# When a new batch's values are computed: after two turned tiles, and ahead of the rows' turns and logits

## What is computed

```python
q = split_heads(x @ Wq + bq); k = split_heads(x @ Wk + bk); v = split_heads(x @ Wv + bv)
p = softmax(where(causal, q @ k.T / sqrt(32) + alibi, min))
x = layernorm(x + (p @ v) @ Wo + bo)
probs = softmax(x @ Wr + br); top_w, top_idx = top_k(probs, 1)
x = layernorm(x + top_w * expert[top_idx](x))      # silu(x @ Wg) * (x @ Wu) @ Wd
```

## Time and profile before

| | |
|---|---|
| median of 3 runs | 1213.38 us (1212.68 to 1215.46) |
| profiled execution | 1214.71 us |
| its span | 1212.9 us |
| mean granted clock of TensorE | 0.976 |
| TensorE busy | 1149.1 us, 95% |
| VectorE, ScalarE, GpSimd busy | 731.5, 590.4, 518.7 us |

### The profile page before, as it was taken

How to read it: one execution, slowest core, us unless ns; L and a number is a source line. 1 busy time by engine, 2 the same in 40 slices (tenths; PEclk the granted TensorE clock), 3 DMA queues, 4 the chain that set the end, 5 groups by cost and what they waited for, 6 DMA issues and landing times.

```text
span 1212.9 us, 25969 instructions
## 1 busy us (share of the span) xinstructions
PE 1149.1 (95%) x7725; PEld 1028.8 (85%) x7725; DVE 731.5 (60%) x1969; ACT 590.4 (49%) x1485; POOL 518.7 (43%) x666
## 2 busy tenths in 40 slices
PE   7899998999999988999999999999999999999994
PEld 5778877887788766989889989989988998998993
DVE  5566676668667746473654565466365456546665
ACT  3588876876787774342333233233232323323354
POOL 6776764755576564630331231133033123213336
PEclk9899998999999988899999999999999999999997
DMA  8323333233332222532222313213222231321312
GB/s 247 101 62 84 67 88 87 54 75 93 84 77 69 71 62 87 176 95 71 71 70 72 105 44 90 77 54 87 71 69 73 71 105 45 95 72 53 88 37 104
DMA packets 105375, 100.12 MB, mean 83 GB/s; under 512 B 10271, under 2 KB 79519, under 8 KB 105248
## 3 DMA queue, kind: packets, MB, share of 16 engines
q1 hardware_dynamic: 100064, 87.18, 26.7%
q0 software_dynamic: 3040, 9.18, 2.4%
q10 hardware_dynamic: 2144, 2.10, 0.6%
HBM read 64.74 MB, written 9.18 MB: 61 GB/s over the span
## 4 chain that ended last, share of the span: by engine, by line
PE 51%; POOL 5%; DMA 2%; issue 2%; DVE 1%; ACT 1%; SPq 0%; POOLq 0%; ACTq 0%; DVEq 0%
PE bank L976 36%; PE bank L1001 9%; POOL up_lo L1735 5%; PE bank L988 3%; DMA up_raw<-in_Wu_dram 2%; PE bank L704 1%; ACT up_hi L1131 1%; PE bank L950 1%; POOL out_dram L1819 0%; DMA y<-x_scratch,row_token 0%; DVE oT_lo L1335 0%; SPq L628 0%; PE bank L803 0%; PE bank L855 0%; PE bank L931 0%
## 5 line engine op out<-in xcount | busy, mean ns | idle before, releaser
L1735 POOL TENSOR_TENSOR up_lo<-up_raw,up_hi 128x256 fp32r<-128x256 f32 x241 | 171.2, 746 | 481.7 <-ACT up_hi L1131 481.3
L976 PE MATMUL bank<-up_hi,xsT_hi 128*128 x1216 | 355.4, 292 | 7.3 <-POOL up_lo L1735 6.3
L976 PE MATMUL bank<-up_hi,xsT_lo 128*128 x1216 | 343.8, 283 | 0.0
L976 PE MATMUL bank<-up_lo,xsT_hi 128*128 x1216 | 343.7, 283 | 0.0
L1543 DVE SCALAR_TENSOR_TENSOR h_tok<-bank,row_weight,silu 128x128 f32<-128x128 f32 x304 | 93.4, 346 | 292.7 <-ACT silu L1233 292.7
L1726 POOL TENSOR_TENSOR pT_lo<-probs,pT_hi 128x512 fp32r<-128x512 f32 (+1 forms) x192 | 210.5, 1103 | 125.4 <-ACT pT_hi L1108 124.4
L976 PEld LDWEIGHTS bank<-up_hi,xsT_hi 128*128 128x128 f32 x1216 | 232.4, 191 | 14.2 <-issue 13.9
L1233 ACT ACTIVATE silu<-bank 128x256 f32<-128x256 f32 (+1 forms) x160 | 59.9, 374 | 364.3 <-PE bank L976 360.6
L976 PEld LDWEIGHTS bank<-up_hi,xsT_lo 128*128 128x128 f32 x1216 | 233.1, 192 | 0.3
L976 PEld LDWEIGHTS bank<-up_lo,xsT_hi 128*128 128x128 f32 x1216 | 232.7, 191 | 0.1
L1560 DVE TENSOR_TENSOR y<-bank,y 128x512 f32<-128x512 f32 x295 | 198.9, 689 | 0.4
(11 more groups left out here) (196 smaller groups left out, 2087.4 us busy)
## 6 DMA issues: line engine op xcount, KB each, us to landing
stack<-qk SPq DMA_DIRECT2D x180, 128.0 KB, 2.4
up_raw<-in_Wg_dram SPq DMA_DIRECT2D x64, 256.0 KB, 3.8
up_raw<-in_Wu_dram SPq DMA_DIRECT2D x64, 256.0 KB, 4.2
down_raw<-in_Wd_dram SPq DMA_DIRECT2D x64, 256.0 KB
x_tok<-in_x_dram SPq DMA_DIRECT2D x16, 256.0 KB, 3.3
x_scratch<-res SPq DMA_DIRECT2D x12, 256.0 KB, 2.4
w_raw<-in_Wo_dram SPq DMA_DIRECT2D x1, 1024.0 KB, 6.5
stack<-max_row SPq DMA_DIRECT2D x64, 2.0 KB
```

What stands on the lines that cost most here:

```text
L976: mm = pe.matmul(bank[:, n * 2 * P:(n + 1) * 2 * P], a[:, s, k, :], up_w[w][k][:, :, :].rearrange("p a f -> p (a f)")[:, bass.ds(at, 2 * P ...
L1735: pool.tensor_tensor(up_w[1][k][:, e, :], up_raw[:, idx % NUPS, k, :, :].rearrange("p g f -> p (g f)"), up_w[0][k][:, e, :].bitcast(F32), ...
```

## The change

In the planner only, and in the waits that follow from it:

- V needs two turned tiles, those of its half, in the place of four (`needs`, and the wait in `tensor`).
- xT needs, in the place of nothing but its x, that the jobs which read the old turned tiles have begun. ScalarE's wait before it overwrites them names both halves of V.
- `turning(u)` is true at a change of batch to 2 or 3, from the moment the first of the four turns has begun until all have. Meanwhile x1t and logit don't start, and the ranks are V and OP 0, xT 0 to 1.75, OT 2, x1t 3, logit 4.
- Otherwise xT's rank grows with its tile, so that tile 0 comes first.

```diff
     def needs(job):
         kind, t = job[0], job[1]
         if kind == "xT":
-            return [("x", t, job[2])]
-        if kind in ("K", "Q", "V"):
-            group = t * 2 if kind == "V" else t
-            return [("read", "xT", group // GPB, k) for k in range(KT)] + [("split", kind)]
+
+            users = [(n, t * GPB - m) for n in ("K", "Q") for m in range(1, GPB + 1)]
+            users += [("V", t * GPB // 2 - m, half) for m in range(1, GPB // 2 + 1) for half in range(2)]
+            return [("x", t, job[2])] + [("begun",) + j for j in users]
+        if kind in ("K", "Q"):
+            return [("read", "xT", t // GPB, k) for k in range(KT)] + [("split", kind)]
+        if kind == "V":
+            return [("read", "xT", t * 2 // GPB, 2 * job[2] + k) for k in range(2)] + [("split", kind)]
...
-                now_job = next((j for j in order if all(k in ready for k in needs(j))), None)
+                now_job = next((j for j in order if all(k in ready for k in needs(j)) and not (j[0] in ("x1t", "logit") and turning(u))), None)
...
+    def turning(u):
+
+        b = min(u // PER_GROUP, NG - 1) // GPB
+        done = [("begun", "xT", b + 1, j) in ready for j in range(QT)]
+        return 0 < b < LAST and any(done) and not all(done)
+
...
-        return {"xT": 0, "OT": 0, "x1t": 1, "logit": 1 if g // GPB == LAST else 4}.get(job[0], 2)
+        if turning(u):
+            return {"OP": 0, "V": 0, "xT": (list(plan.number)[-1][0] in ("xT", "x1t", "OT")) + job[-1] / QT, "OT": 2, "x1t": 3, "logit": 4}.get(job[0], 0)
+        if job[0] == "xT":
+            return job[2] / QT
+        return {"OT": 0, "x1t": 1, "logit": 1 if g // GPB == LAST else 4}.get(job[0], 2)
...
-                        pe.wait_ge(s_side_dve, xT_count[t * 2 // GPB])
+                        pe.wait_ge(s_side_dve, max(done("xT", t * 2 // GPB, 2 * half + k) for k in range(2)))
...
-                        act.wait_ge(s_side, max(done("K", t * GPB - 1), done("Q", t * GPB - 1), done("V", t * GPB // 2 - 1, 1)))
+                        act.wait_ge(s_side, max(done("K", t * GPB - 1), done("Q", t * GPB - 1), done("V", t * GPB // 2 - 1, 0), done("V", t * GPB // 2 - 1, 1)))
```

More of the change, by code:

```diff
@@ L173, in make_plan @@
         plan.flushed[job] = 0
-    ready = {("begun", "OP", -1), ("begun", "logit", -1)} | {("x", b, j) for b in range(2) for j in range(QT)} | {("read",) + job for job in first}
+    ready = {("begun", "OP", -1), ("begun", "logit", -1)} | {("x", b, j) for b in range(2) for j in range(QT)} | {(what,) + job for job in first for what in ("begun", "read")}
     queue, left, now_job, pending, later, over = deque(), [], None, [], deque(), 0
```

## The result

The changed kernel takes 1218.06 us (median of 22 runs) where the kernel before, run beside it, takes 1213.82 us (22 runs). The ratio of the runs is 1.0027 with a 95% interval of 1.0015 to 1.0038: slower by 3.3 us, between 1.8 and 4.6 (the plain medians are 4.2 us apart; I go by the ratio, which has an interval). Put on the 1213.38 us from which the prediction started, that is 1216.7 us. The profiled execution of the changed kernel took 1218.62 us, with a span of 1216.8.

A forecast was written before the change was run, and what follows sets the result against it. TensorE, busy for 95% of the span, was taken to bound the kernel. First, second and third change and clock, -0.2 + 1.3 + 1.5 - 1.2 = +1.4 us on 1213.4, gave 1214.8 us, range 1211.2 to 1217.4.

The forecast's parts named there:

- no difference that can be told: Whole kernel: time within 0.2% (about 2.4 us) of the unchanged one, with a lean to slower; chance 0.65.
- rival 1: Steps 94 to 98 and 142 to 146: new half-clock stretch, 1.7 to 3.4 us each, 1216.5 to 1218.2 us; chance 0.23.
- What the clock gives back: Behind the second batch change's long wait: denser products raise the clock sooner, -1.2 us on the median; third change 0.
- "wrong" line: Signs against the forecast, among them a low-clock stretch as long as now despite dense products, giving 1216.0 us.
- Long waits: TensorE's 2.97 us waits at the second and third batch changes, and 1.54 us at the first, stay: worth 0.
- First change: Change to batch 1: the wait before the values' first product goes from 0.87 to about 0.65 us, -0.2 us.
- Second change: Steps 94 to 97: work moved earlier leaves TensorE waiting on DMA, losing 1.1 to 1.5 us, taken as 1.3.
- Third change: Steps 142 to 145: the place can't be passed before 335.46 us, so 1.5 us turns into a wait.
- Who is late: Behind Q's take, six stack loads delay the row of maxima, so turned scores wait; possibly the scores of step 96 earlier.
- Rival 2: New DMA waits at 227 and 335 us don't come because the loads are hidden anyway: 1212.0 us; chance 0.15.
- 3: Clock gains its upper end: 1212.1 us with the forecast waits (chance 0.07), 1209.3 us without them (0.04).
- 4: One 2.97 us wait goes because takes shift, and its low-clock stretch with it: 1210.1 us; chance 0.03.

The follow-up runs named there:

- after: The changed kernel with the whole change, against the kernel without it: 1218.06 us, ratio 1.0027.
- before: The kernel without the change, run beside the changed kernel: 1213.82 us.
- the shifted kernel: The changed kernel plus sixteen short idle products (128x128) in the wait of step 133, so TensorE's code loads earlier: 1214.44 us, 0.9985 of the unchanged kernel.
- third change alone: The unchanged kernel with the new needs and order at the change to batch 3 only: 1218.60 us, ratio 1.0020.
- after once more: The changed kernel run again, unaltered, for a second profile: 1223.93 us, 1.0054 of the kernel without the change.
- before with idle products: The unchanged kernel plus eight idle products (128x512, results overwritten) in front of each 2.97 us wait: 1211.13 us, ratio 0.9971.
- with the normalisation moved: The unchanged kernel with VectorE's row normalisation put behind the mask and biased maxima of its step: 1205.46 us, ratio 0.9915.
- first alone: The unchanged kernel with the new needs and order at the change to batch 1 only: 1215.49 us, ratio 1.0007.
- second alone: The unchanged kernel with the new needs and order at the change to batch 2 only: 1219.12 us, ratio 1.0027.
- after with idle products: The changed kernel plus eight idle products before each long wait, four and eight before the stack-load waits: 1213.98 us, 0.9979 of the unchanged kernel.
- after with the normalisation moved: The changed kernel with VectorE's row normalisation put behind the mask and biased maxima: 1210.58 us, 0.9960 of the kernel without the change.

## Why the prediction was right, and where not

- **The sum.** Forecast +1.4 us with a lean to slower, measured +3.3 (1.8 to 4.6). On the 1213.38 us base that is 1216.7, inside the range of 1211.2 to 1217.4, near its upper end. What did not hold is "no difference that can be told": the loss of 0.27% (0.15 to 0.38) lies over the prediction's own line of 0.2%, a case that it gave 0.28. The terms without the clock made -0.2 + 1.3 + 1.5 = 2.6 us. Measured at equal clock: 2.7 to 3.1. This part held. That nothing more came on top is in part luck: the clock, which the sum had at -1.2, came out at about nothing over the runs, although rival 1 came too.
- **What the clock gives back, -1.2 us, is the term that failed.** The step was "could rise from about 207 us on": it did in the profile of after. But the prediction's own "wrong" line said what if not, 1216.0 us, and that is nearly what came. One profile of before was taken as its usual low stretch, while both plans draw from a wide spread: over 195 to 215 us the clock was 0.74, 0.74 and 0.83 in three profiles with the old order there, and 0.83 five times and 1.00 once with the new one. That looks like a gain; over all runs, though, no saving of lost clock is seen. At the third change the new order loses clock behind its load wait, where three profiles show 1.8 to 3.2 us (head 46 to 48 against the shifted kernel, less the difference of the waits). Whether a real saving behind the long waits stands against it, or only the draw of a few profiles, stays open. The term also took a lost microsecond at its full price; over the runs it costs 0.77.
- **Long waits.** 2.97 us twice and 1.54 us, unchanged: right.
- **First change.** 0.87 to 0.65 us: right to the hundredth; in time -0.2 by the milestones, untellable in the runs (+0.8, between -1.3 and 3.2).
- **Second change, 1.3 us.** The milestones give 1.1 to 1.3 us at equal clock (third change alone, which has the old order here, 29.76; after, after once more and the shifted kernel 31.04, 30.94, 30.81, all at 0.83) and 1.8 at full clock (28.96 and 28.91 against 27.11). At equal clock the runs say 2.8 ± 0.5. The size was right at low clock and 0.5 us short at full clock. Missing in the sum was the 0.5 us ahead of the values' first product, which waits for the take of the second tile of a pair and is hidden only where the clock is low.
- **Third change, 1.5 us.** 1.15 us by itself; the runs at equal clock say 1.7 ± 0.5. On top came 0.75 to 1.2 us by the code transfer (waits of 1.39, 1.43 and 1.85 against 0.64), for which the prediction had no term, only an end: "if they come later by half a microsecond".
- **Who is late.** Right that SyncE's row of loads behind Q's take sets the place: waits for it of 0.88 and 1.85 us, 25.0 and 23.8 us behind the long ones, where 1.1 to 1.8 and some 27 were forecast. Wrong in which: not the turned scores and the row of maxima, but a step earlier the scores of heads 32 and 48, for the third of the six loads. The prediction had called that possible with the same sum. The rule of the Trainium skill that it quoted ("DMA: Bandwidth & Descriptors", issue early and wait late) held: the computing taken away from under the loads turned into 0.88 us of waiting. The fixed 2 us that it took from the same page are stated there for DMAs that GpSimd issues; these are SyncE's, of 128 KB, and landed 2.4 us behind the start of their issue where nothing disturbed them.
- **Rival 1, a new stretch at half clock (0.23).** It came in steps 142 to 146 and not in 94 to 98, and cost 1.8 to 3.2 us, its price of 1.7 to 3.4. Its condition was too loose: thin steps and a wait of over 1 us did not suffice at 1.16 and 1.18 us at the second change, and did at 1.39 at the third. **Rival 2 (loads hidden), 3 and 4**: none came; the waits are there in every profile of this order.

The three changes taken alone add up to 2.0 us more at equal clock than all of them together (0.6 + 2.8 + 1.7 = 5.1, against 3.1), with a standard error of about 1.0. I can't say whether that is scatter.

## What to carry to other kernels

Work that is moved ahead of a row of loads leaves the loads bare: look at what covered them. Where a machine's clock falls behind a wait, one profile gives one draw of its length; compare kernels by milestones at equal clock, by many runs with their clock beside them, or with idle work in the wait that takes the clock out. And cost the longest wait's cause before reordering around it: here one instruction moved behind another on VectorE was worth three times what the change lost.

## What the runs showed of the hardware

- **A code transfer lengthens a DMA issue.** I read the six loads behind Q's take at the third change in all fourteen profiles. Where the 0.02 MB transfer fell among them the longest issue took 0.83 to 1.80 us (eight profiles, those of before with idle products or with the normalisation moved among them, where no wait for the loads came of it); where it fell elsewhere, at most 0.67 (six: before, first alone, second alone, after with idle products, the shifted kernel, after with the normalisation moved). Landing then came up to 3.7 us behind the start, where it is 2.4 undisturbed. With sixteen short products more on TensorE the transfer fell elsewhere, the longest issue was 0.67 us, and the wait 0.64. Reordering one engine's work can thus slow another engine's DMA. How the transfer holds the issue up is not shown.
- **Lost clock costs 0.77 of itself** in time (223 runs). That part of each low stretch lies in waiting would explain it; no run shows the reason.
- **Idle products are cheap insurance**: 2.09 us of them inside a 2.97 us wait at both later changes gave 3.5 us (1.1 to 5.9), and the mean lost clock went from 29.1 to 22.4 us. A wait of 1.07 us in front of them was left, with the clock at 1.00 behind it. The Trainium skill ("TensorE: Matmul & The Clock Gate", section "What's actually happening") says that the number of slow products differs between runs of one kernel; the profiles here agree: two of the same changed kernel have 1.00 and 0.93 of the clock over 300 to 325 us, and 0.89 and 0.77 over 330 to 345.
